# Own rows written tile by tile, and window sums in front of the transposes, in a graph layer with an expert layer

## The reference

```
xn  = layernorm(x)
agg = segment_sum((xn[src] @ W_rel[type] + b_rel[type]) * weight, dst) / max(degree, 1)
x1  = layernorm(xn + xn @ W_self + b_self + agg) * g1 + b1
ffn = gelu(x1 @ W_ffn1 + b_ffn1) @ W_ffn2 + b_ffn2
x   = x + layernorm(x1 + ffn) * g2 + b2
xm  = layernorm(x)
out = x + sum over the two best experts e of  p_e * (gelu(xm @ w1_e.T + b1_e) @ w2_e.T + b2_e)
```

## Time and profile before

| | us |
|---|---|
| time, median of 3 runs (675.43 to 677.49) | 677.15 |
| the profiled execution's own time | 674.45 |
| its span in the trace | 672.5 |
| TensorE busy in matmuls | 529.1 |
| VectorE busy | 318.8 |
| GpSimd busy | 231.2 |
| ScalarE busy | 118.5 |

### The profile page before, as it was taken

The page is one execution under the profiler, slowest core; times in us unless marked ns, Lnnn a source line. Parts: engine busy times, 40 slices in busy tenths (PEclk is TensorE's granted clock), DMA queues, the critical chain, the costliest instruction groups (busy, mean ns, idle before and its releaser), DMA issues.

```text
span 672.5 us, 7258 instructions
## 1 busy us (share of the span) xinstructions
PE 529.1 (79%) x2292; PEld 356.9 (53%) x2293; DVE 318.8 (47%) x845; ACT 118.5 (18%) x250; POOL 231.2 (34%) x269
## 2 busy tenths in 40 slices
PE   1799999999960199999999999934728889989500
PEld 1588888887610165565665757522226656666300
DVE  5596573212300714598695999567401122222144
ACT  0501001000110032232322222112003222222000
POOL 2740000037676057777677200000730011110173
PEclk9999999969976589999999999965558999999955
DMA  8454242247699047777676288070542487783286
GB/s 286 180 167 162 95 156 94 94 128 210 195 401 393 1 121 209 202 195 203 175 203 196 78 321 335 1 314 2 208 182 91 132 310 249 246 284 112 70 247 214
DMA packets 47538, 125.47 MB, mean 187 GB/s; under 512 B 6336, under 2 KB 6976, under 8 KB 45200
## 3 DMA queue, kind: packets, MB, share of 16 engines
q0 software_dynamic: 17344, 63.20, 30.3%
q1 hardware_dynamic: 26912, 54.95, 21.8%
q10 hardware_dynamic: 3248, 6.89, 3.4%
HBM read 85.70 MB, written 39.32 MB: 186 GB/s over the span
## 4 chain that ended last, share of the span: by engine, by line
PE 69%; issue 9%; POOL 7%; DVE 6%; DMA 6%; ACT 2%; ACTq 1%; POOLq 0%; SPq 0%; DVEq 0%
PE ps L814 11%; PE ps L825 9%; PE ps L947 7%; PE ps L754 7%; PE ps L755 7%; PE ps L756 7%; PE ps L964 7%; PE ps L780 5%; POOL greg L563 3%; POOL xslot L537 3%; PE ps L940 2%; POOL greg L516 2%; DMA w_in<-w_rel 2%; PE ps L791 2%; DMA greg<-xslot 1%
## 5 line engine op out<-in xcount | busy, mean ns | idle before, releaser
L516 POOL DMA_INDIRECT greg<-msg,row_i x157 | 155.3, 989 | 178.5 <-DMA msg<-greg 101.5
L754 PE MATMUL ps<-w_hi,xT_hi 128*128 128x512 f32 x200 | 80.7, 403 | 1.7 <-DVE xT_lo L1041 1.7
L755 PE MATMUL ps<-w_lo,xT_hi 128*128 128x512 f32 x200 | 80.0, 400 | 0.0
L756 PE MATMUL ps<-w_hi,xT_lo 128*128 128x512 f32 x200 | 80.0, 400 | 0.0
L814 PE MATMUL ps<-freg,wreg 128*128 128x256 f32 x320 | 71.5, 382 | 0.8 <-ACT freg L613 0.8
L825 PE MATMUL ps<-wreg,freg 128*128 128x512 f32 x160 | 72.1, 598 | 0.0
L814 PEld LDWEIGHTS ps<-freg,wreg 128*128 128x128 f32 x320 | 60.1, 190 | 16.3 <-issue 7.5
L947 PE MATMUL ps<-wreg,freg 128*128 x224 | 55.3, 391 | 0.0
L964 PE MATMUL ps<-wreg,freg 128*128 x112 | 52.8, 593 | 0.9 <-ACT freg L700 0.9
L780 PE MATMUL ps<-greg,sel 128*32 128x512 f32 x320 | 46.2, 636 | 5.8 <-DMA greg<-msg,row_i 5.8
L537 POOL DMA_INDIRECT xslot<-work,pos_i x20 | 19.7, 986 | 85.5 <-DVE pos_i L1318 79.8
(11 more groups left out here) (170 smaller groups left out, 645.7 us busy)
## 6 DMA issues: line engine op xcount, KB each, us to landing
wreg<-experts POOLq DMA_DIRECT2D x11, 1025.0 KB, 6.2
msg<-greg SPq DMA_DIRECT2D x40, 256.0 KB, 2.0
xslot<-greg SPq DMA_DIRECT2D x1, 8960.0 KB, 25.5
greg<-xslot SPq DMA_DIRECT2D x28, 256.0 KB, 3.7
yslot<-greg SPq DMA_DIRECT2D x28, 256.0 KB, 2.4
wreg<-experts SPq DMA_DIRECT2D x5, 1025.0 KB, 9.7
wreg<-w SPq DMA_DIRECT2D x8, 512.0 KB, 12.8
w_in<-w_rel ACTq DMA_DIRECT2D x3, 1024.0 KB, 6.1
```

What stands on the lines that cost most here:

```text
L516: nc.gpsimd.indirect_dma_start(gath[:, c % RING, :], None, msg, bass.IndirectOffsetOnAxis(ap=row_i[:, c:c + 1], axis=0)).then_inc(s_gath[c ...
L754: nc.tensor.matmul(bank(t % 5), xT_hi[:, at], w_hi[:, i, wk], start=(k == 0), stop=False)
L755: nc.tensor.matmul(bank(t % 5), xT_hi[:, at], w_lo[:, i, wk], start=False, stop=False)
L756: mm = nc.tensor.matmul(bank(t % 5), xT_lo[:, at], w_hi[:, i, wk], start=False, stop=(k == KD - 1))
```

## The change

Three edits. First, SP writes the own rows tile by tile: for each tile it waits until DVE has added that tile's self product, and issues one DMA of 256 KB; all ten stand in SP's program ahead of the weight loads, where one DMA of all ten tiles stood behind them. DVE's wait ahead of the first norm of tile 0 counts all ten. Second, on PE `window_sums(n)` stands in front of `turn_x1(p)`, where it stood behind it. Third, the same on ACT: `sums_out(n)` in front of `copy_x1T(p)`.

```diff
@@ SP @@
+            for t in range(NT):
+                sp.wait_ge(s_evac, FREE + NT * REL + t + 1)
+                sp.dma_start(own_rows[t * P:(t + 1) * P, :], work[:, t, :]).then_inc(s_own, 16)
             sp.wait_ge(s_prod, NT * (REL + 1))
             for k in range(KD):
                 sp.dma_start(w1_v[:, k, :], w1[k * P:(k + 1) * P, :]).then_inc(s_ffw, 16)
             for k in range(0, KF, 2):
                 sp.dma_start(w2_v[:, k:k + 2, :],
                              w2[k * P:(k + 2) * P, :].rearrange("(k p) n -> p k n", p=P)).then_inc(s_ffw, 16)
-            sp.wait_ge(s_evac, FREE + NT * (REL + 1))
-            sp.dma_start(own_rows.rearrange("(t p) d -> p t d", p=P), work[:, :, :]).then_inc(s_own, 16)
-
             sp.wait_ge(s_zeros, 1)
@@ ACT @@
             for p in range(PAIRS):
                 n = 4 * p + 5
-                copy_x1T(fast, p)
                 if n < STEPS:
                     sums_out(n)
+                copy_x1T(fast, p)
                 gelu(fast, p, 0, 4)
@@ PE @@
             for p in range(PAIRS):
                 n = 4 * p + 5
-                turn_x1(fast, p)
                 if n < STEPS:
                     window_sums(n)
+                turn_x1(fast, p)
                 hidden(fast, p, 0, 4)
@@ DVE @@
                 if s == 3:
-                    dve.wait_ge(s_own, 16)
+                    dve.wait_ge(s_own, 16 * NT)
                     fast_first_norm(0)
```

## The result

| | before | after |
|---|---|---|
| median, us (4 runs each) | 676.29 (674.59 to 677.49) | 655.66 (653.91 to 657.77) |
| profiled execution, its span | 674.45, 672.5 | 653.97, 652.2 |

The ratio is 0.9698, 95% interval [0.9653, 0.9743]: 3.0% faster, 20.6 us, where 657.7 us and 19.4 us less were forecast.

What follows compares the result with a forecast made beforehand. PE, 69% of the chain, was taken as the bound, with a 22.80 us hole before pair 0. Gain 25.3 - 2.0 (clock) - 3.9 (pairs 1 to 3) = 19.4; 677.15 - 19.4 = 657.7 us, range 652.0 to 664.5.

Steps and rivals of the forecast that it cites:

- Part 1: Own rows tile by tile: DVE's first norm of tile 0 no longer waits for their copy, starting 21.4 us earlier.
- Charging nothing for the writes: Self product: ten tile writes beside the gathers bring DMA engines to 0.90, under a full queue's 1.04, so 0 us lost.
- Part 2: Start of pair 0: hidden product 25.3 us earlier, of which 21.4 own rows, 1.0 `add_windows(4)`, 2.8 swap; clock loss separate.
- The term of the clock: Pair 0's hidden product runs partly at half clock after PE's wait: 2.0 us lost, bounds 0 to 3.8.
- Part 3: Pairs 1 to 3: PE idles 1.3 us each while ACT makes four copies in a row; 3.9 us lost.
- (a): Pairs 1 to 3: the swap is free or nearly, a later PE wait absorbing the idle; 653.9 us; chance 0.12.
- (b): Ahead of pair 0: another wait, such as weights landing at 218.4, replaces much of the copy's; 667.9 us; chance 0.10.
- (c): Self product: writes halve the gathers' rate and PE waits for them; 10.6 us slower, 687.8 us; chance 0.03.
- (d): First norm: own-row copies no quicker in pieces, DVE waits as before, only the swap remains; 678.3 us; chance 0.03.

Runs made afterwards that it cites:

- kernel 1: Kernel before with only the own rows written tile by tile, PE and ACT in the old order; 651.97 us against 674.84, ratio 0.9654.
- kernel 2: Kernel before with only the swap on PE and ACT, own rows still one copy behind the weight loads; 680.21 us against 674.84, ratio 1.0076.
- experiment 5: The changed kernel timed again, unaltered; 655.67 us against 674.15 for the kernel before, ratio 0.9721.
- experiment 6: The changed kernel without the copy of the own rows and without DVE's wait for it; 655.22 us, ratio 0.9737 to the kernel before.
- experiment 4: The changed kernel with the own rows as one DMA in front of the weight loads; 663.75 us, ratio 0.9813 to the kernel before.
- kernel 3: The changed kernel with the swap in pair 0 alone, old order in pairs 1 to 3; 652.09 us, ratio 0.9642 to the kernel before.
- first two calls: Two timing sessions, each of four experiment kernels beside the kernel before, which took 674.84 and 674.15 us.
- kernel 7: The changed kernel with ACT in the old order and PE in the new; 651.99 us, ratio 0.9666 to the kernel before.
- third call: Session timing the change, kernel 1, kernel 3 and kernel 7 again beside the kernel before (702.26 us); ratios 0.9837, 0.9808, 0.9796 and 0.9816.
- first call: Session timing kernel 1, kernel 2, kernel 3 and experiment 4 beside the kernel before, which took 674.84 us.

## Why the prediction was right

**Part 1, own rows.** Predicted 21.4 us to the first norm, measured 23.4. The mechanism is shown by experiments 1 and 2: with the own rows alone the norm starts at 195.25, with the swap alone it waits until 215.53. Of the 2.0 us more, 1.3 were there at the last tile of the self product (179.48 for 180.79), with a higher clock in 139 to 150 (0.69 for 0.60), before the first own row was written; that is chance, for in the same kernel's second profile, experiment 5, the tile is summed at 180.66 and the norm starts at 196.72. From that tile to the norm it is 22.0 us less for the 21.4 forecast. The weights landed at 205.1 where 206.9 was reckoned: 1.3 us of that is again the earlier self product. PE's wait for them, 1.39 us, lay beneath DVE's norm as foreseen. Charging nothing for the writes was right as far as the times can tell (experiment 6), and the share of DMA that they added, 0.19, is close to the 0.21 of the estimate; that each gather would take 1.4 us longer beside them wasn't foreseen. The Trainium skill's page "DMA: Bandwidth & Descriptors" ("Queues, rings and completion order") says that descriptors in one ring are taken in order. The traces agree: the last weights land at 205.7 with the copy behind them, 205.1 with it cut up and 205.4 without it (kernel 6), and in experiment 4, with it whole in front, at 216.6, for 7.0 us of waiting.

**Part 2, pair 0.** `add_windows(4)` at full clock gave 0.9 us for 1.0. From `x1` to the hidden product 1.3 us for the 1.8 predicted, because the four transposes ran at full clock (0.66 for 1.11). The term of the clock, 2.0 us lost, was 0 in the first profile. It isn't wrong as a mechanism: the first 32 rows of the hidden product took 7.2, 9.6 and 8.9 us in the change, its repeat and kernel 6, 10.1 in kernel 2 and 8.8 in kernel 3. So it is 0 to 3 us from one profile to the next, 0 and 2.4 in the two of the change, and 2.0 was a fair middle.

**Part 3, pairs 1 to 3.** Predicted 3.9 us lost. Measured 4.0 from pair 0 to pair 4. The forecast's 1.3 us for each is what pair 3 shows, 4.10 - 2.82 = 1.28, of which 1.15 is idle time. That the total fits as well is in part luck, for two things that weren't in the sum cancel. The sums of step 8 took 2.39 us here for 1.92 elsewhere. And from pair 1 to pair 2 the hidden products are only 0.9 us further apart than before (44.9 for 44.0), for 1.4 from pair 2 to pair 3 (44.9 for 43.5): half a microsecond of one gap comes back. From pair 1 to pair 4 the kernels of the first two calls and the change lose 2.3 us with the full swap on both engines, 1.4 with it on PE alone and 0 without it. Taking the swap's two sides together, from `x1` of tile 1 to pair 4's hidden product, the trace has 171.1 us in kernel 1, 172.7 in the change, 175.1 in its repeat: it costs 1.5 to 3.9 us as a whole. Experiment 2 has it as a time, 0.8% slower, some 5 us, a little more than the traces show.

**The sum.** 19.4 forecast, 20.6 measured. Two terms were off in the kind direction (2.0 of the first norm, 2.0 of the clock) and one, the 3.3 us lost behind pair 4, was not in the sum at all. Part of the closeness is luck.

**The rivals.** (a), the swap is free, is out by experiment 3's and 1's pairs, though half a microsecond of it came true. (b), weights in the place of the copy, doesn't happen in the change, but is just what kernel 4 does: 0.9813. (c) and (d) are out by experiment 6 and by the landings of at most 4.8 us.

**The best version.** Kernels 1, 3 and 7 lie at 0.964 to 0.967 of the time before, the change at 0.970 and 0.972. The traces give a reason, the gaps; the times alone don't separate all of them. So the whole gain is that of the own rows, and the swap of the other two edits adds none that a time shows.

## What to carry to other kernels

A write that nobody reads soon still has a reader: whoever may overwrite its source. Look for the semaphore that guards it, and cut the write along the loop that makes the data, so that it goes out while the queue has room; moved in front of the loads in one piece it only hands its lateness to them. Work that stands between a producer and the consumer of its copy is cover: where PE is already busy all the time, moving it away opens a gap per iteration. Only in the iteration that had a wait to fill did it bring anything, 2.4 us in the trace of kernel 3, and there the lower clock took 1.6 back.

## What the runs showed of the hardware that was not expected

The granted clock at the start of pair 0 isn't the same from one execution to the next: 1.00 in 216 to 220 in the first profile of the change, 0.53 in its second, with the same instructions and nearly the same idle time of PE ahead of the last transposes (1.91 and 2.10 us), worth 2.4 us in 32 rows. And the third call ran all kernels some 27 us slower (702.26 us for the kernel before, for 674 to 676 elsewhere), with stops of up to 13.5 us on several engines at once. Its chip has the same number on record, 14, as that of the first call, where the kernel before took 674.84 us, so the chip isn't shown to be the cause.
